# Two-layer window network with a sorted mixture of experts on one Trainium2 core: the scatters of a tile split around GpSimd's powers, the experts' weights prepared inside the first tiles

## The reference, cut to what matters

```python
# layer 1, on xn = layernorm(x), in windows of 7 x 7 pixels
w  = ln(windows(xn), ln1_w, ln1_b)
h  = x_B[step] + h @ A            # over the 49 pixels of a window, x_B = w @ Bm
xr = h @ Cm
y  = gelu(ln(xr, ln2_w, ln2_b) @ W1 + b1) @ W2 + b2      # 96 -> 384 -> 96
x2 = x + xr + y
# layer 2, on t = layernorm(x2)
p    = softmax(t @ gate_w + gate_b)                       # 4 experts
keep the two largest, divide them by their sum (+1e-9)
out  = x2 + sum_e p_e * (gelu(t @ w1_e + b1_e) @ w2_e + b2_e)
```

## Time and profile before

| | |
|---|---|
| Median of 3 runs | 1978.55 us (1976.9 to 1979.15) |
| Profiled execution: time, span | 1976.8 us, 1975.1 us |
| TensorE busy | 1880.0 us, 95% of the span |
| VectorE, ScalarE, GpSimd busy | 1487.9, 1601.9, 1361.3 us |
| First half (first record of the MLP to the last scatter) | about 54 to 959 us |
| Second half | about 965 to 1975 us |

### The profile page before, as it was taken

The page is one execution under the profiler, slowest core; times in us unless marked ns, Lnnn a source line. Parts: engine busy times, 40 slices in busy tenths (PEclk is TensorE's granted clock), DMA queues, the critical chain, the costliest instruction groups (busy, mean ns, idle before and its releaser), DMA issues.

```text
span 1975.1 us, 36825 instructions
## 1 busy us (share of the span) xinstructions
PE 1880.0 (95%) x8981; PEld 1311.6 (66%) x8981; DVE 1487.9 (75%) x6675; ACT 1601.9 (81%) x3068; POOL 1361.3 (69%) x1094
## 2 busy tenths in 40 slices
PE   3999999999999999997499999999999999999996
PEld 2566666666666666664377777777777777777774
DVE  5677787778777877776377777777777777777775
ACT  3787878877887788785399999999999998999995
POOL 2277667666766676667467777777777777777775
PEclk9999999999999999999699999999999999999998
DMA  5022222222222222111566666666666666666662
GB/s 181 19 72 66 65 66 72 67 67 66 72 66 68 66 70 66 62 50 50 193 202 207 201 210 207 215 206 207 202 208 211 211 209 204 203 212 210 213 208 76
DMA packets 121095, 272.93 MB, mean 138 GB/s; under 512 B 26085, under 2 KB 34686, under 8 KB 120883
## 3 DMA queue, kind: packets, MB, share of 16 engines
q1 hardware_dynamic: 85680, 209.91, 34.9%
q0 software_dynamic: 32000, 58.87, 8.6%
q10 hardware_dynamic: 3202, 1.80, 0.4%
HBM read 204.47 MB, written 66.98 MB: 137 GB/s over the span
## 4 chain that ended last, share of the span: by engine, by line
PE 91%; ACT 3%; issue 2%; POOL 2%; DMA 1%; DVE 1%; ACTq 0%; SPq 0%; POOLq 0%; DVEq 0%
PE y_ps L994 13%; PE mix_ps L1113 7%; PE mix_ps L1114 7%; PE mix_ps L1115 7%; PE mix_ps L1026 5%; PE turn_ps L973 4%; PE mix_ps L1013 4%; PE mix_ps L1020 4%; PE turn_ps L1099 4%; PE up_ps L1099 4%; PE turn_ps L1100 4%; PE turn_ps L1101 4%; PE up_ps L1100 4%; PE up_ps L1101 4%; PE tok_ps L1122 3%; PE up_ps L985 3%
## 5 line engine op out<-in xcount | busy, mean ns | idle before, releaser
L458 POOL DMA_INDIRECT out<-out_sb,idx x412 | 425.5, 1033 | 266.5 <-DVE out_sb L918 157.7
L874 DVE TENSOR_TENSOR g_lo<-g,g_hi 128x512 fp32r<-128x512 f32 x618 | 424.1, 687 | 200.2 <-ACT g_hi L588 200.0
L431 POOL DMA_INDIRECT sorted_rows<-rows,pos x392 | 382.4, 975 | 118.9 <-issue 104.2
L588 ACT CAST g_hi<-g 128x512 fp32r<-128x512 f32 x618 | 380.8, 616 | 13.1
L447 POOL TENSOR_TENSOR ex<-euler,rows 128x16 f32<-128x16 f32 x103 | 305.3, 2964 | 9.7 <-DMA rows<-sorted_rows 9.3
L994 PE MATMUL y_ps<-g,d_mlp 128*100 128x512 f32 x588 | 295.4, 597 | 9.1 <-ACT y_sb L535 8.5
L1113 PE MATMUL mix_ps<-g_hi,ew 128*96 128x512 f32 x618 | 244.4, 396 | 0.3 <-DVE g_lo L874 0.2
L1114 PE MATMUL mix_ps<-g_hi,ew 128*96 128x512 f32 x618 | 244.2, 395 | 0.0
L1115 PE MATMUL mix_ps<-g_lo,ew 128*96 128x512 f32 x618 | 244.0, 395 | 0.0
L526 ACT ACTIVATE g<-up_ps 128x512 f32<-128x512 f32 x294 | 172.9, 605 | 68.3 <-PE up_ps L987 67.8
L985 PE MATMUL up_ps<-y_hi,w_hi 98*128 98x512 f32 x294 | 214.7, 730 | 1.8 <-DVE y_lo L793 1.8
(11 more groups left out here) (177 smaller groups left out, 4175.4 us busy)
## 6 DMA issues: line engine op xcount, KB each, us to landing
ew<-expert_w SPq DMA_DIRECT2D x206, 384.0 KB, 4.1
ew<-expert_w SPq DMA_DIRECT2D x206, 288.5 KB, 3.6
rows<-sorted_rows SPq DMA_DIRECT2D x103, 394.0 KB
x_in<-in_x SPq DMA_DIRECT2D x49, 384.0 KB, 3.0
out<-out_sb,idx POOLq DMA_INDIRECT x412
sorted_rows<-rows,pos POOLq DMA_INDIRECT x392, 2.5
sorted_rows<-pad_rows SPq DMA_DIRECT2D x11, 394.0 KB, 4.8
expert_w<-w_hi SPq DMA_DIRECT2D x4, 192.0 KB, 2.1
```

The costliest lines, as they stand in the source:

```text
L431: pool.indirect_dma_start(out=sorted_rows[:, :], out_offset=bass.IndirectOffsetOnAxis(ap=pos[:, r, s:s + 1], axis=0), in_=rows[:, r, s, :] ...
L458: pool.indirect_dma_start(out=out_rows, out_offset=bass.IndirectOffsetOnAxis(ap=idx[:, r, s:s + 1], axis=0), in_=out_sb[:, r, s, :], in_of ...
L588: act.copy(g_hi[:, n % PART_RING, :], g[:, n % G_RING, :]).then_inc(hi_done, 1)
L874: dve.tensor_tensor(g_lo[:, n % PART_RING, :], g[:, n % G_RING, :], f(g_hi[:, n % PART_RING, :]), ALU.subtract).then_inc(lo_done, 1)
```

## The change

- `scatter(p-2)` is issued in two groups, three before the two powers and five behind them; only the second group waits for ScalarE's part of the rows. The second power covers only those of its two halves that are in use.
- `positions(p-2)` on VectorE stands behind the statistics of the rows of tile p−1, ahead of the statistics of x.
- The rank matmuls take fp32r operands; `count` is fp32r.
- `up(p, 5)` stands ahead of `down(p, 3)` on TensorE.
- The experts' weights are loaded by ScalarE's queue in period −2 and split in periods 0 (up part, ScalarE), 1 (its remainder on VectorE, down part on ScalarE) and 2 (remainder of the down part on VectorE). The bias part of the experts is made in period −1. SP stores all of it once the last part is there; the load of x for tile 5 goes ahead of the stores, those from tile 6 on stay behind.
- The zeroing of `w_hi`, `w_lo` and `y_hi` goes from VectorE to GpSimd, behind its first power; the first weights wait for four loads instead of eight and treat only the MLP's 384 bias columns; the bias rows are moved by SP's queue; SP loads two tiles of x ahead of them and three behind; ScalarE runs one small gelu at the start; the gate's products stand in period −2.
- In the second half VectorE copies `pair_of` ahead of `t_lo(0)` and the first `part_lo`.

```diff
-FIRST_LOADS, MLP_LOADS, LATER_LOADS = 8, 3, 2
+FIRST_LOADS, GATE_LOADS, MLP_LOADS, LATER_LOADS = 4, 4, 3, 2
+X_FIRST = 2
+FIRST_SUBS = 3
...
-        count = sb("count", [P, TYPES, SUBS])
+        count = sb("count", [P, TYPES, SUBS], F32R)
... (SP)
-            for t in range(X_RING):
+            for t in range(X_FIRST):
+                load_x(t)
+            sp.wait_ge(prep, 3)
+            sp.dma_start(b_aug[C:C + 1, 0:C], b_row[:, COL_B:COL_W1]).then_inc(bias_rows, 16)
+            sp.wait_ge(zeroed, 2)
+            sp.wait_ge(prep, 7)
+            sp.dma_start(f(w_hi[C:C + 1, 0:HID]), f(b_hi[:, 0:HID])).then_inc(bias_rows, 16)
+            sp.dma_start(f(w_hi[C + 1:KR, 0:HID]), f(b_lo[:, 0:HID])).then_inc(bias_rows, 16)
+            for t in range(X_FIRST, X_RING):
                 load_x(t)
...
+            load_x(X_RING)
+            sp.wait_ge(later_prep, 4)
+            sp.wait_ge(later_rows, 32)
             for e in range(EXPERTS):
... (the 20 stores)
-            for t in range(X_RING, TILES):
+            for t in range(X_RING + 1, TILES):
                 load_x(t)
... (GpSimd)
+                which = slice(0 if tile(t) else 1, 2 if tile(t - 4) else 1)
-                pool.tensor_tensor(rstd_xt[:, t % 2, :, :], var_eps[:, LN_X:, :], neg_half[:, :, :], ALU.pow).then_inc(rstd_xt_ok, 1)
+                pool.tensor_tensor(rstd_xt[:, t % 2, which, :], var_eps[:, 1 + which.start:1 + which.stop, :],
+                                   neg_half[:, which, :], ALU.pow).then_inc(rstd_xt_ok, 1)
...
-                    pool.wait_ge(t_n_ok, t + 1)
+                if subs[-1] >= HALF_SUBS:
+                    pool.wait_ge(t_n_ok, t + 1)
...
             for p in periods():
+                if tile(p - 2):
+                    scatter(p - 2, range(FIRST_SUBS))
                 if tile(p + 1):
                     rstd_of_r(p + 1)
                 if tile(p + 3) or tile(p - 1):
                     rstd_of_x_and_t(p + 3)
                 if tile(p - 2):
-                    scatter(p - 2, range(SUBS))
+                    scatter(p - 2, range(FIRST_SUBS, SUBS))
+                if p == -3:
+                    pool.wait_ge(rstd_xt_ok, 1)
+                    pool.memset(f(w_hi[C:P, :]), 0.0).then_inc(zeroed, 1)
+                    pool.memset(f(w_lo[C:P, :]), 0.0).then_inc(zeroed, 1)
+                    pool.memset(f(y_hi[C:KR, :]), 1.0).then_inc(zeroed, 1)
+                    pool.wait_ge(zeroed, 3)
... (ScalarE)
+            act.activation(y_sb[0:C, 0, 0:EXPERTS], a_aug[:, C:CG], ACT.Gelu)
...
-                if p == -3:
-                    biases()
-                    expert_parts()
                 if tile(p):
                     copy_y(p, 1)
+                if p == -2:
+                    load_experts()
+                if p == 0:
+                    expert_up_parts()
+                if p == 1:
+                    expert_down_parts()
... (VectorE, the loop over periods; new order around the change)
                     variance(LN_T, p - 1, (rstd_xt_ok, p + 3))
+                if tile(p - 2):
+                    positions(p - 2)
                 if tile(p + 3):
...
                 if p == -3:
+                    scaled_weights()
                     first_weights()
-                    centred_weights()
-                if p == -1:
-                    later_weights()
+                if p == -2:
+                    gate_columns()
+                    rank_weights()
...
                     shift_of_r(r)
-                if tile(p - 2):
-                    positions(p - 2)
...
                     shift_of_x(p + 3)
+                if p == -3:
+                    centred_weights()
+                if p == -1:
+                    expert_biases()
+                if p == 1:
+                    expert_up_lows()
+                if p == 2:
+                    expert_down_lows()
                 if tile(p - 1):
                     shift_of_rows(p - 1)
... (VectorE, second half: the two copies of pair_of move ahead of this)
             t_lo(0)
             for n in range(AHEAD):
                 part_lo(n)
... (TensorE)
-                    pe.matmul(tok_ps[:, 0:TYPES], earlier[:, :], count[:, :, SUBS - 1], start=True, stop=True)
+                    pe.matmul(tok_ps[:, 0:TYPES], earlier_r[:, :], count[:, :, SUBS - 1], start=True, stop=True)
...
                     up(p, 4)
+                    up(p, 5)
                     down(p, 3)
-                    up(p, 5)
...
+                if p == -2:
+                    gate_products()
```

More of the change, by code:

```diff
@@ L304, in _ @@
             sp.wait_ge(later_prep, 2)
-            sp.wait_ge(act_prep, 2)
-            sp.wait_ge(bias_rows, 48)
+            sp.dma_start(f(w_hi[C:C + 1, HID:]), f(b_hi[:, HID:])).then_inc(later_rows, 16)
+            sp.dma_start(f(w_hi[C + 1:KR, HID:]), f(b_lo[:, HID:])).then_inc(later_rows, 16)
+            load_x(X_RING)
+            sp.wait_ge(later_prep, 4)
+            sp.wait_ge(later_rows, 32)
             for e in range(EXPERTS):
@@ L627, in _, with scaled_weights @@
             dve.memset(var_eps[:, :, :], 1.0).then_inc(ones_set, 1)
-            dve.memset(f(w_hi[C:P, :]), 0.0).then_inc(ones_set, 1)
-            dve.memset(f(w_lo[C:P, :]), 0.0).then_inc(ones_set, 1)
             dve.memset(x_t[C:C + 1, :], 1.0).then_inc(ones_set, 1)
-            dve.memset(f(y_hi[C:KR, :]), 1.0).then_inc(ones_set, 1)
-            def first_weights():
+            def scaled_weights():
                 dve.wait_ge(first_loaded, 16 * FIRST_LOADS)
@@ L662, in centred_weights, with rank_weights, expert_biases, expert_up_lows @@
                     "p (k e) -> p k e", k=KB)).then_inc(gate_sums, 1)
-            def later_weights():
+            def rank_weights():
+                dve.wait_ge(const_step, CONSTS)
+                dve.tensor_copy(earlier_r[:, :], earlier[:, :]).then_inc(rank_ones, 1)
+                dve.tensor_copy(ones_r[:, :], ones[:, :]).then_inc(rank_ones, 1)
+                dve.tensor_copy(vec[:, 0, :], tau7[:, :])
+            def expert_biases():
+                dve.tensor_copy(b_hi[:, HID:], b_row[:, COL_E:]).then_inc(later_prep, 1)
+                dve.wait_ge(later_prep, 1)
+                dve.tensor_tensor(b_lo[:, HID:], b_row[:, COL_E:], f(b_hi[:, HID:]), ALU.subtract).then_inc(later_prep, 1)
+            def expert_up_lows():
+                dve.wait_ge(act_prep, 1)
+                dve.wait_ge(zeroed, 3)
+                dve.tensor_tensor(w_lo[0:C, HID:], w_raw[:, COL_E:], f(w_hi[0:C, HID:]), ALU.subtract).then_inc(later_prep, 1)
+            def expert_down_lows():
                 dve.wait_ge(act_prep, 2)
-                dve.tensor_tensor(w_lo[0:C, HID:], w_raw[:, COL_E:], f(w_hi[0:C, HID:]), ALU.subtract).then_inc(later_prep, 1)
                 dve.tensor_tensor(d_lo[:, :, :], d_raw[:, :, :], f(d_hi[:, :, :]), ALU.subtract).then_inc(later_prep, 1)
@@ L779, in positions @@
                 dve.tensor_tensor(base[:, :], tok_ps[:, TYPES:2 * TYPES], base[:, :], ALU.add).then_inc(base_set, 1)
-                dve.tensor_tensor(place[:, :, :], count[:, :, :], offset[:, :].unsqueeze(2).to_broadcast([P, TYPES, SUBS]),
+                dve.tensor_tensor(place[:, :, :], f(count[:, :, :]), offset[:, :].unsqueeze(2).to_broadcast([P, TYPES, SUBS]),
                                   ALU.add).then_inc(pos_step, 1)
@@ L930, in _ @@
                             mix_ps[:, BANK:BANK + (BLOCKS + 1) * EXPERTS]).then_inc(pair_ok, 1)
+            t_lo(0)
+            for n in range(AHEAD):
+                part_lo(n)
             dve.wait_ge(pair_ok, 2)
@@ L959, in _, with gate_products @@
             pe.wait_ge(const_step, CONSTS)
+            pe.wait_ge(gate_loaded, 16 * GATE_LOADS)
             pe.matmul(mix_ps[0:C, 0:EXPERTS], ones[0:C, 0:C], gate_raw[:, :], start=True, stop=True).then_inc(gate_sums, 1)
[L961 to L969, removed]
+            def gate_products():
+                pe.wait_ge(gate_sums, 2)
+                pe.wait_ge(mlp_loaded, 16 * MLP_LOADS)
+                gw = b_aug[0:C, C:CG]
+                at = lambda n: slice(BANK + n * EXPERTS, BANK + (n + 1) * EXPERTS)
+                pe.matmul(mix_ps[0:C, at(0)], turned[:, 0:C], gw, start=True, stop=True)
+                for k in range(KB):
+                    pe.matmul(mix_ps[:, at(1 + k)], turned[:, C + k * P:C + (k + 1) * P], gw, start=True, stop=True)
+                pe.matmul(mix_ps[0:CG, BANK + (1 + KB) * EXPERTS:BANK + (1 + KB) * EXPERTS + 1], b_aug[0:C, :], b2_col[0:C, 0:1],
+                          start=True, stop=True).then_inc(gate_sums, 1)
             def to_channels(src):
@@ L1038, in _ @@
                     tok.take(pe, base_set, p - 1)
+                    pe.wait_ge(rank_ones, 2)
                     pe.wait_ge(score_counted, p - 1)
-                    pe.matmul(tok_ps[:, 0:TYPES], earlier[:, :], count[:, :, SUBS - 1], start=True, stop=True)
```

(3 more changed lines are left out.)

49 lines of the change are left out of this document (24 added, 25 removed).

## The result

The changed kernel takes 1985.66 us (median of 7 runs, 1984.25 to 1986.8), the kernel before 1978.2 us (median of 7, 1976.83 to 1979.15). The ratio is 1.0038, with a 95% interval of 1.0027 to 1.005: slower, by 7.5 us. The forecast was 1987. The span of the profiled execution grew from 1975.1 to 1985.1 us, by 10.0 where the sum had +9.8. The profiled execution of the changed kernel is the slowest of its seven (1986.8 us), that of the kernel before lies 1.3 us under its median, so the 10.0 is somewhat more than the 7.5 between the medians.

What follows compares the result with a forecast made beforehand. It saw TensorE nearly full in a middle tile, with ScalarE and VectorE loops also closing there. −12.0 + 1.9 + 6.2 + 3.2 + 13.9 − 3.4 = +9.8 us on 1976.8 gave 1986.6, stated as 1987, range 1979 to 1994.

Steps and rivals of the forecast that it cites:

- The tile: Tiles 2 to 45: early positions exceed the VectorE loop's spare 0.86 us, +0.33 us a tile, 13.9 us in all.
- Rival 1: Middle tile: the VectorE loop has room, so the rank saving shows, 42 × −0.22 = −9.2 us; 1963.5; chance 0.18.
- up(5): TensorE, up(5) ahead of down(3): worth 0, since down(5) waits for gelu 5; bound 0.37 us of gain a tile.
- Scatters in three and five: GpSimd in each tile: three scatters ahead of the power for xr end 0.3 us before it is wanted, no cost.
- rival 4: GpSimd: the three scatters are slow, each 0.3 us longer, 42 × 0.6 = +25 us, 2012; chance 0.04.
- The seam: Start of the second half: pair_of copied first removes TensorE's 3.09 us wait, scatters give 0.3; −3.4 us (−7 to −1).
- Period 3: Load of x for tile 6 waits behind the stores: +6.2 us, and slow TensorE records after the idle time add 3.2.
- rival 2: Load of tile 6 comes in time, no stall and no fall of the clock: −9.4 us, 1977; chance 0.12.
- The start: Before the first T0: zeroing on GpSimd, four loads waited for, fewer bias columns; −12.0 us (−15 to −8).
- Rival 3: The start gains 4 us in place of 12, bias rows waiting for GpSimd's zeroing and SP's queue; 1995; chance 0.12.
- period 2: Tile 2: the experts' up remainder on VectorE makes y_lo 1.75 us late, +1.9 us (+0.4 to +2.5).

Runs made afterwards that it cites:

- The square: Middle tiles compared with positions late or early: 18.02 and 18.53 us with rank products in two passes, 17.76 and 18.30 us in one.
- experiment 2: Changed kernel with all eight scatters in one group behind the powers, positions left early: 1982.88 us, ratio 1.0027.
- experiment 1: Changed kernel with positions back behind shift_of_r and the eight scatters in one group behind the powers: 1959.76 us, ratio 0.9909.
- experiment 5: Changed kernel with up(5) back behind down(3): 1985.05 us, ratio 1.0036.
- experiment 3: Kernel before with only positions ahead of the statistics of x and scatters in three and five: 2003.24 us, ratio 1.0128.
- experiment 8: Kernel before with only VectorE's two copies of pair_of ahead of the first remainders in the second half: 1972.91 us, ratio 0.9974.
- experiment 6: Changed kernel with three loads of x instead of one ahead of the stores: 1974.56 us, ratio 0.9987.
- experiment 11: Changed kernel with positions late, scatters in one group, three loads of x ahead of stores, gelu 5 ahead of xr_n, GpSimd's fills first: 1946.64 us, ratio 0.9839.
- experiments 4: Changed kernel with the rank products in two passes (fp32) again: 1995.32 us, ratio 1.0091.

## Why the prediction was right, and where its terms were off

**The tile: right, and shown.** The chain through VectorE, GpSimd and ScalarE was said to have 0.86 us to spare and `positions` to bring in 1.11. Measured: 18.30 us a tile against 18.35. ScalarE waits 0.42 us for `shift_r` (said about 0.5), GpSimd 0.32 for the variance (said under 0.5), and `shift_x` waits 0.31 us for the second power, which nobody feels. The square and experiment 2 show that it is an effect of `positions` alone: 0.54 us against the single-pass tile of 17.76. The term came to 11.8 instead of 13.9.

**Rival 1 fell, by its own condition.** It needed `xr_n` to start no later than behind gelu 4. In the changed kernel ScalarE waits there in every middle tile, in experiment 1 in none, and there the tile falls by 0.26, the rank saving that this rival priced at 0.22.

**`up(5)`: right.** Worth 0 with positions early (experiment 5), for the reason given: a TensorE gap moves from `down(3)` to `down(5)`. With positions late, where TensorE is busy 17.65 of 17.76 us, its worth was not tested.

**Scatters in three and five: right in a middle tile, not in the seam.** In a middle tile 0 (experiment 2); the mean scatter stays at 0.98 us, so rival 4 fell. In the seam the split costs something: in the changed kernel the one group (experiment 2) has 1055.8 us from the last T0 to the end, the two groups 1057.5. Early positions cost another 2.2 there (experiment 1 has 1053.6, experiment 2 1055.8). In the kernel before the two edits together cost 5.6 (experiment 3); that run doesn't separate them. The last tiles have no x any more, and the changed kernel's second power covers only 8 values a partition then:

```profile
952.26 1.68 POOL L437 TENSOR_TENSOR rstd_xt<-var_eps,neg_half 128x8 f32<-128x8 f32 x1
```

1.7 us instead of the 2.9 of the 16-value form. I read the costs as GpSimd's powers of the last tiles standing behind three scatters with no x to work on in between; that reading was not tested by a run of its own.

**The seam: net right, by luck in its parts.** −3.6 against −3.4. The order of `pair_of` gives as much as all of it (−3.7, experiment 8; said −3.1). Experiment 1 has the rest of the changed seam without early positions and split, and is 3.8 us shorter again (1053.6 against 1057.4); the shorter power is the likely cause, not shown by itself. The positions (+2.2) and the split (+1.7) take that back, where the prediction took a single gain of 0.3.

**Period 3: right in its mechanism, the stall too small.** Counted from the T0 before (74.86), the load of tile 6 goes out at +30.1 (104.9) as said (the remainder was 0.6 us earlier, the stores took 10.7 us instead of 10.0). The rest was off in one direction: it lands 5.4 us later, not 3.4,

```profile
DMA to landing us min/median/max: 5.4/6.5/7.0
```

(line L298, loads of x issued from 100 to 112 us) and VectorE stands ready at 102.69, 1.0 us sooner than the +28.8 of the forecast. 4.7 + 2.0 + 1.0 = 7.7, the wait in the row.

The prediction took its 3.1 us from the earlier trace rows, and one of those two loads, at 42.88, also went out directly behind the 20 stores. So the place in the queue doesn't make a load slow. What differs is how full the DMA engines are while the stores run, first in the kernel before, then in the changed one (DMA share and GB/s are the last two numbers):

```profile
33.00:43.00 10.00, 7.07 (x26) 4.96 (x25) 3.28 (x20) 2.45 (x5) 1.12 (x1) 1.00 0.82 275
94.30:104.90 10.60, 10.60 (x53) 6.86 (x52) 7.95 (x45) 8.59 (x18) 5.26 (x7) 1.00 0.98 284
```

From 94 to 105 us GpSimd's scatters run beside the stores, which they didn't before, and take part of these engines:

```profile
q0 software_dynamic: 240, 0.50, 14.1%
```

Moving the stores into the tiles put them there. That the scatters are what slows the load is argued from these shares; no run left them out.

With the slow records behind it periods 3 and 4 cost 10.7 us where 6.2 + 3.2 = 9.4 stood. Three loads ahead of the stores take 9.7 us of it back (experiment 6), so rival 2's "no stall" was worth what it said; its condition just wasn't met. The size of the stall is not exact to the us: in the six kernels with one load ahead of the stores period 3 takes 27.71 to 29.39 us.

**The start: the step that was mis-sized.** −9.4 us at the first T0, −10.3 with period 0, where −12.0 stood. The weights start at 6.69, as said (6.7), but x is normalised at 13.86, not at 11.0, and `from_input` follows at 21.46, not at 18.9. The prediction moved VectorE's zeroing to GpSimd and counted it as hidden; two of VectorE's casts then last 1.8 us each beside it, where 0.34 and 0.35 were possible (experiment 11 has both). That is 2.9 us, the whole difference. Where only one is held (experiments 4, 5 and 6), the start with period 0 gives −12.4, −11.2 and −12.7. Rival 3, a gain of only 4 through the bias rows, fell.

**Errors that cancelled.** The start (+2.6 us, +1.7 with period 0) and the stall (+1.3) were worse than said, the tile (−2.1) and period 2 (−0.6) better. The sum was also added to the profiled time (1986.6) and not to the median (1978.55 + 9.8 = 1988.4); the 1987 stands between. So the closeness of +9.8 to +10.0, and of 1987 to 1985.66, is partly chance; the sign isn't, since the tile term alone is 11.8 and can be switched off.

## What to carry to other kernels

A bound engine at 99% doesn't say that only it sets the period: find each loop that closes on the next iteration, count its slack in microseconds, and hold it against what an edit puts into it; here 1.1 us of small VectorE work went into a loop with 0.86 us to spare, and a kernel that could have been 1.6% faster became 0.4% slower. When work is made later and a queue waits for it, look at what stands behind it in that queue: one loop bound from 1 to 3 was worth 10 us. Test the parts of a change one by one, as a good part (the single pass, −0.25 us a tile) can hide behind a bad one (+0.54).

## What the runs showed of the hardware that was not expected

- The cast of 96x384 values takes 0.34 us alone and 1.80 us when it starts beside GpSimd's fill of 32x1920; the cast of a single row of 384 takes 0.35 and 1.82. A fill, which only writes, was enough. Which of the two engines comes first changed between kernels whose start is the same, with a load that landed up to 0.5 us sooner, and together they moved everything behind by 2 us.
- The scatters took 0.98 us each in the mean, placed three ahead of the powers beside VectorE's statistics or all behind them. This doesn't test the same lock: between 200 and 900 us of the changed kernel no cast or copy of VectorE runs beside a scatter.
- 9.2 us of idle TensorE were followed by records at 0.50 of the granted clock (the turning in 1.92 us, 1.04 elsewhere), while the same stretch without the idle time shows 1.00.
- A load of x directly behind the 20 stores landed in 3.1 us with the DMA engines 82% busy and nothing but SP's queue on them, and in 5.4 us at 98%, with scatters beside.
